# Edge loops of a graph kernel in trips of two iterations, extra sums for every second group, eight raw groups

## The reference

```python
def _gcn(x, W, b, src, dst, w, n):
    h = x @ W
    agg = jax.ops.segment_sum(w[:, None] * h[src], dst, num_segments=n)
    return agg + b

h = _gcn(f1, W1, b1, src, dst, values, N)
root1 = f1[root_idx[batch]]
x = _leaky(jnp.concatenate([h, root1], axis=1))
x = _leaky(_gcn(x, W2, b2, src, dst, values, N))
root2 = f2[root_idx[batch]]
x = _leaky(jnp.concatenate([x, root2], axis=1) @ Wl + bl)
```

## Time and profile before

| | |
|---|---|
| Median of three runs | 2652.09 us (2641.73 to 2658.28) |
| Profiled execution, its own time | 2650.82 us |
| Its span | 2649.1 us |
| Mean granted clock of PE | 0.84 |
| First layer's edge loop with node steps (first to last stage) | 110.8 to 1268.0 us |
| Second layer's | 1334.2 to 2574.8 us |

### The profile page before, as it was taken

How to read it: one execution, slowest core, us unless ns; L and a number is a source line. 1 busy time by engine, 2 the same in 40 slices (tenths; PEclk the granted TensorE clock), 3 DMA queues, 4 the chain that set the end, 5 groups by cost and what they waited for, 6 DMA issues and landing times.

```text
span 2649.1 us, 39172 instructions
## 1 busy us (share of the span) xinstructions
PE 1820.2 (69%) x7140; PEld 1432.8 (54%) x7141; DVE 1141.4 (43%) x3987; ACT 375.1 (14%) x939; POOL 1507.6 (57%) x1580
## 2 busy tenths in 40 slices
PE   0476656666656666565478788888878778777886
PEld 0354445444444444444256666666657566565664
DVE  6443333333333332333245445455444444444456
ACT  5200000000000000000011111111211112111121
POOL 3566565666566666665555556565656655666620
PEclk9988788877777678777678899998889888898887
DMA  7733233333233333332222222222222222222312
GB/s 240 234 91 88 85 89 87 89 89 91 87 89 95 93 87 97 93 95 83 80 72 73 77 81 81 77 83 81 81 77 81 85 81 79 81 81 83 87 32 97
DMA packets 113292, 242.23 MB, mean 91 GB/s; under 512 B 28934, under 2 KB 62661, under 8 KB 113259
## 3 DMA queue, kind: packets, MB, share of 16 engines
q0 software_dynamic: 75200, 205.10, 27.0%
q1 hardware_dynamic: 30094, 29.04, 3.4%
q10 hardware_dynamic: 7964, 7.76, 0.9%
HBM read 222.42 MB, written 19.38 MB: 91 GB/s over the span
## 4 chain that ended last, share of the span: by engine, by line
PE 28%; issue 26%; DVEq 19%; DVE 16%; another core or an unknown queue 8%; ACT 2%; DMA 1%; POOL 0%; ACTq 0%
PE ps_agg L573 17%; DVE S L942 6%; PE ps_dn L678 4%; DVEq L942 3%; PE ps_up L689 3%; DVE acc L950 2%; DVEq L964 2%; DVE S_more L942 2%; DVEq L973 2%; DVEq L950 2%; DVEq L977 1%; DVEq L948 1%; DVEq L986 1%; DVEq L949 1%
## 5 line engine op out<-in xcount | busy, mean ns | idle before, releaser
L573 PE MATMUL ps_agg<-ring,S 128*128 x3136 | 886.7, 433 | 377.5 <-DVE acc L950 278.4
L326 POOL DMA_INDIRECT ring<-conv_rows,idx x782 | 755.7, 966 | 537.6 <-DVEq L972 294.9
L326 POOL DMA_INDIRECT ring<-normed_rows,idx x760 | 725.5, 955 | 484.9 <-DVEq L972 231.6
L573 PEld LDWEIGHTS ps_agg<-ring,S 128*128 128x128 f32 x3136 | 663.1, 218 | 544.1 <-issue 442.3
L942 DVE TENSOR_SCALAR S<-iota,dstc,wc 128x128 f32<-128x128 int16 x1584 | 457.8, 354 | 310.5 <-issue 286.8
L950 DVE TENSOR_TENSOR acc<-acc,ps_agg x490 | 206.3, 421 | 872.3 <-remote 421.0
L573 PE MATMUL ps_agg<-ring,S_more 128*128 x768 | 254.2, 488 | 264.8 <-DVE S_more L942 175.7
L573 PEld LDWEIGHTS ps_agg<-ring,S_more 128*128 128x128 f32 x768 | 179.2, 244 | 328.7 <-issue 298.6
L678 PE MATMUL ps_dn<-fw2s,hT 128*128 128x256 f32 x848 | 228.3, 428 | 0.0
L678 PEld LDWEIGHTS ps_dn<-fw2s,hT 128*128 128x128 f32 x848 | 177.7, 216 | 49.3 <-issue 22.0
L689 PE MATMUL ps_up<-xnT,fw1s 128*128 128x256 f32 x800 | 190.5, 392 | 4.3 <-ACT hT L443 4.3
(11 more groups left out here) (195 smaller groups left out, 1026.0 us busy)
## 6 DMA issues: line engine op xcount, KB each, us to landing
ring<-conv_rows,idx POOLq DMA_INDIRECT x782
ring<-normed_rows,idx POOLq DMA_INDIRECT x760
xs<-in_x SPq DMA_DIRECT2D x6, 1280.0 KB
conv_rows<-rows ACTq DMA_DIRECT2D x50, 128.0 KB
out_rows<-xs SPq DMA_DIRECT2D x6, 896.0 KB
normed_rows<-xs SPq DMA_DIRECT2D x4, 1280.0 KB, 5.2
xs<-in_x SPq DMA_DIRECT2D x4, 1152.0 KB
normed_rows<-xs SPq DMA_DIRECT2D x1, 1152.0 KB, 4.8
```

The lines of the kernel that those rows point to most:

```text
L326: pool.indirect_dma_start(out=ring[:, slot * TG + t, :], out_offset=None, in_=rows_of, in_offset=bass.IndirectOffsetOnAxis(ap=idx[:, tile: ...
L573: last = nc.tensor.matmul(to, select[:, t, :], moving, start=(t == 0), stop=(t == TG - 1))
```

## The change

- **Trips of two.** One iteration (`first_turn`, `edge_round` with b = 0) stands ahead of the loop, and the loop makes 24 trips of two iterations. The two halves of the ring, the PSUM bank, and the places of S are then constants of the code. Semaphores are one for each group of an iteration (`s_ready[q]`, `mm_done[q]`, `acc_done[q]`) and count iterations, so that their values are the same for all four groups. The four table entries of an iteration are read together. DVE copies the iteration's columns of destinations and weights to `cols`, from where S is made without a computed address.
- **Extras for every second group.** Extras of groups 0 and 1 are done in one loop behind group 1, those of 2 and 3 behind group 3: on PE after the piece of the node step, on DVE before it. They use bank 0, and DVE waits in this loop for PE's matmuls. Groups 0 and 2 on PE wait until the extra's sum is added (`x_added`).
- **POOL** waits once for eight gathers (`acc_done[q + 1]`), not once for four.
- **The start.** RAWG is 8: the whole ring (30 tiles) is gathered raw. POOL normalises 14 tiles of the input's rows and 14 of the raw tiles, ACT 35 and 16. The tables are computed before the rows' statistics, the first edge iteration runs before the root's term, and the rows' stores go ahead of the weights' loads on SP. The last node step of the first layer stands behind the loops.

```diff
-    RAWG = 6
+    RAWG = 8
...
-        dstc = sb("dstc", [P, PADT + NT])
-        wc = sb("wc", [P, PADT + NT])
-        dmore = sb("dmore", [P, TG])
+        dw = sb("dw", [P, 2, PADT + NT])
+        dstc = dw[:, 0, PADT:PADT + NT]
+        cols = sb("cols", [P, 2, 2, RING])
+        xcols = sb("xcols", [P, 2, TG])
...
-        XCH = [(39, NW), (29, 39), (20, 29), (10, 20), (0, 10)]
+        XCH = [(39, NW), (29, 39), (19, 29), (14, 19), (7, 14), (0, 7)]
+        BY_POOL = range(4, len(XCH))
...
-        s_ready = [sem(f"s_ready{l}") for l in L2]
-        more_ready = [sem(f"more_ready{l}") for l in L2]
-        mm_done = [sem(f"mm_done{l}") for l in L2]
-        acc_step = [sem(f"acc_step{l}") for l in L2]
-        group_used = [sem(f"group_used{l}") for l in L2]
+        s_ready = [sem(f"s_ready{q}") for q in range(QG)]
+        mm_done = [sem(f"mm_done{q}") for q in range(QG)]
+        acc_done = [sem(f"acc_done{q}") for q in range(QG)]
+        first_cols, cols_ready = sem("first_cols"), sem("cols_ready")
+        x_copied, x_ready, x_done, x_added = sem("x_copied"), sem("x_ready"), sem("x_done"), sem("x_added")
...
                     if l == 0 and g == RAWG:
+                        pool.wait_ge(stats_ready, 2)
+                        for c in BY_POOL:
+                            for w in range(*XCH[c]):
+                                last = nc.gpsimd.tensor_scalar(xs[:, X0 + w, :], xs[:, X0 + w, :], rstd[:, w:w + 1], nmr[:, w:w + 1], ALU.mult, ALU.add)
+                            last.then_inc(f_pool, 1)
+                        pool.wait_ge(raw_stats, 1)
+                        for t in RAW_TILES[0]:
+                            last = nc.gpsimd.tensor_scalar(ring[:, t, :], ring[:, t, :], raw_rstd[:, t:t + 1], raw_nmr[:, t:t + 1], ALU.mult, ALU.add)
+                            if t % TG == TG - 1 or t == RAW_TILES[0][-1]:
+                                last.then_inc(raw_first, 1)
                         for stored in f_stored:
                             pool.wait_ge(stored, 16)
-                    if g >= SLOTS:
-                        pool.wait_ge(group_used[l], g - SLOTS + 2)
+                    if it >= 2 and q % 2 == 0:
+                        pool.wait_ge(acc_done[q + 1], it + NIT * l)
...
             zero(NW // 2, NW)
+            zero(0, NW // 2)
             normalise_rows(0)
-            zero(0, NW // 2)
             normalise_rows(1)
-            normalise_raw(0)
-            for stored in f_stored:
-                act.wait_ge(stored, 16)
-            act.wait_ge(root_ready, 1)
-            r = within(act.value_load(rooti[0:1, 2:3]), N - 1)
-            act.dma_start(rootcol[:, :], f_dram[ds(r, 1), :].rearrange("o (k p) -> p (k o)", p=P)).then_inc(rootcol_loaded, 16)
-            normalise_raw(1)
+            act.wait_ge(raw_stats, 2)
+            for t in RAW_TILES[1]:
+                last = nc.scalar.activation(ring[:, t, :], ring[:, t, :], ACT.Identity, scale=raw_rstd[:, t:t + 1], bias=raw_nmr[:, t:t + 1])
+            last.then_inc(raw_second, 1)
...
+            def sums(bank, select, moving):
                 for t in range(TG):
...
+                    last = nc.tensor.matmul(ps_agg[:, bank, 0:D], select[:, t, :], moving(t), start=(t == 0), stop=(t == TG - 1))
+                return last
+            def group(q, b, n, gathered):
+                added = within(pe.snap(items), ITEMS, 1) if q % 2 == 0 else None
+                pe.wait_ge(landed[b][q], gathered[q])
+                pe.wait_ge(s_ready[q], n(0))
+                pe.wait_ge(acc_done[(q + 2) % QG], n(0 if q < 2 else 1))
+                if q % 2 == 0:
+                    pe.wait_ge(x_added, added)
+                sums(q & 1, S[:, q, :, :], lambda t: ring[:, b * RING + q * TG + t, :]).then_inc(mm_done[q], 1)
+            def more_sums(q, b, n, spans):
+                first, count = spans
+                with pe.If(0 < count):
+                    with pe.Fori(0, count) as j:
+                        i = within(pe.snap(items), ITEMS, 1)
+                        second = within(pe.snap((j + (SLOT + 1) - first) >> CBITS), 1)
+                        at = within(pe.snap(second * TG + (b * RING + (q - 1) * TG)), SLOTS * TG - TG)
+                        pe.reg_mov(items, i + 1)
+                        pe.wait_ge(acc_done[q - 1], n(1))
+                        pe.wait_ge(x_ready, i)
+                        pe.wait_ge(x_added, i)
+                        sums(0, S_more, lambda t: flat(ring[:, t:SLOTS * TG - TG + 1 + t, :][:, ds(at, 1), :])).then_inc(x_done, 1)
+            def turn(b, n, row, gathered, steps=None, step=None):
+                _, entries = nc.values_load_multi_w_load_instructions(
+                    wtab[0:1, ds(row, QG)], engines=(mybir.EngineType.PE,), min_val=0, max_val=ENTRY, skip_runtime_bounds_check_because="the tables it comes from hold clamped values")
+                more = [within(pe.snap(v >> CBITS), NW - 1) for v in entries]
+                spans = {q: (more[q - 1], within(pe.snap(more[q - 1] + more[q]), 2 * NW - 2)) for q in (1, 3)}
+                for q in range(QG):
+                    group(q, b, n, gathered)
+                    if steps:
+                        steps[q](*step)
+                    if q in spans:
+                        more_sums(q, b, n, spans[q])
...
+                turn(1, n, row, [odd] * QG, steps, step[0])
+                n2 = Count(pe, n(1))
+                row2 = within(pe.snap(m * (-2 * QG) + QG * (NIT - 3)), NG - QG)
+                turn(0, n2, row2, [even] * (QG - 1) + [short], steps, step[1])
...
-            def select(ready, to, dst_of, tile):
+            half, step = dve.alloc_register("dve_half_lag"), dve.alloc_register("dve_step")
+            items, pend = dve.alloc_register("dve_items"), dve.alloc_register("pending_slot")
+            def select(ready, to, of):
 
                 for t in range(TG):
-                    column = within(dve.snap(tile + t), PADT + NT - 1)
-                    at = dstc[:, ds(column, 1)] if dst_of is None else dst_of[:, t:t + 1]
-                    last = V.tensor_scalar(to[:, t, :], iota[:, 0:P], at, wc[:, ds(column, 1)], ALU.is_equal, ALU.mult)
+                    last = V.tensor_scalar(to[:, t, :], iota[:, 0:P], of[:, 0, t:t + 1], of[:, 1, t:t + 1], ALU.is_equal, ALU.mult)
                 last.then_inc(ready, 1)
 
-            def add_last(l, i):
...
+            def add(slot, bank, done):
+                to = flat(acc[:, ds(slot, 1), :])
+                V.tensor_tensor(to, to, ps_agg[:, bank, 0:D], op=ALU.add).then_inc(done, 1)
+            def add_group(q, n, slot):
+                added = within(dve.snap(items), ITEMS, 1) if q % 2 else None
+                dve.wait_ge(mm_done[q], n(0))
+                dve.wait_ge(acc_done[(q - 1) % QG], n(0 if q == 0 else 1))
+                if q % 2:
+                    dve.wait_ge(x_added, added)
+                add(slot, q & 1, acc_done[q])
+            def add_pending(n):
+                add_group(QG - 1, Count(dve, n(-1)), within(dve.snap(pend), A0 + NW - 1, A0))
+            def more_sums(q, n, col, slots, spans):
+                first, count = spans
+                with dve.If(0 < count):
+                    with dve.Fori(0, count) as j:
+                        i = within(dve.snap(items), ITEMS, 1)
+                        dve.reg_mov(items, i + 1)
+                        second = within(dve.snap((j + (SLOT + 1) - first) >> CBITS), 1)
+                        mask = within(dve.snap(second * SLOT), SLOT)
+                        down = within(dve.snap(j - (first & mask)), NW - 1)
+                        tile = within(dve.snap(second * TG + (col + (q - 1) * TG)), PADT + NT - TG)
+                        below = within(dve.snap((slots[q - 1] & (mask * -1 + SLOT)) + (slots[q] & mask)), A0 + NW - 1, A0)
+                        slot = within(dve.snap(below - 1 - down), A0 + NW - 1, A0)
+                        V.tensor_copy(xcols[:, 1, :], dw[:, 1, ds(tile, TG)])
+                        V.tensor_scalar(xcols[:, 0, :], dw[:, 0, ds(tile, TG)], shifts[:, ds(down, 1)], None, ALU.add).then_inc(x_copied, 1)
+                        dve.wait_ge(x_copied, i)
+                        select(x_ready, S_more[:, :, :], xcols)
+                        dve.wait_ge(x_done, i)
+                        dve.wait_ge(x_added, i)
+                        dve.wait_ge(acc_done[q - 1], n(1))
+                        add(slot, 0, x_added)
+            def edge_round(l, n, b, row, col, steps=None, s=None):
+                if not isinstance(row, int):
+                    add_pending(n)
+                if steps:
+                    dve.wait_ge(acc_done[QG - 1], n(0))
+                    dve.sem_inc(window_ready[l], 1)
+                _, entries = nc.values_load_multi_w_load_instructions(
+                    wtab[0:1, ds(row, QG)], engines=(mybir.EngineType.DVE,), min_val=0, max_val=ENTRY, skip_runtime_bounds_check_because="the tables it comes from hold clamped values")
```

(20 more changed lines are left out.)

464 lines of the change are left out of this document (227 added, 237 removed).

## The result

The changed kernel is **slower**: 2837.57 us (median of four runs, 2811.31 to 2847.92) against 2648.45 us, a ratio of 1.070 (95% interval 1.061 to 1.078). The forecast was 2363 us. The profiled execution took 2834.91 us.

A forecast was written before the change was run, and what follows sets the result against it. It took register, branch and semaphore instructions, slowed to 0.7 us during long gather runs, to bound the edge loops. Terms -130 - 121 - 12 - 25 = -288 took 2650.8 us to 2363 us; 8-in-10 range 2185 to 2530.

The forecast's parts named there:

- the price of the slow stretches: Edge loops: in long gather runs each non-computing instruction costs DVE and PE some 0.7 us instead of 0.07.
- 13 slow instructions: First layer: some 13 instructions of 0.69 us form the path during about 9 of an iteration's 24.1 us.
- The term for POOL's wait for eight gathers: POOL's release wait: halves the waits, makes each later by one group; at worst 3.0 us pause behind every eight.
- The extras: Second layer: DVE stands at extras behind PE's FFN piece, delaying normalisation and zT; 24 x 1.6 = +38 us.
- Rival D: Second layer's extras behind the FFN piece make the kernel slower: 2810 us, or 2760 in a smaller form; chance 0.05.
- Its smaller form: Edge loops: POOL pauses 3.0 us behind every eight gathers, giving 26 us an iteration and 2760 us.
- Its larger form: Second layer: each of 48 extras exposes FFN piece and normalisation, 6.8 + 3.3 us, together 485 us; 2810 us.
- Rival C: Loop jumps: the sums' unnamed waits, 5.2 us each, are the price of a trip; halved trips give 2408 us; chance 0.07.
- Rival A: Edge loops: POOL sets the pace throughout, 20.3 and 21.0 us an iteration, 2194 us; chance 0.22.
- The start: Before the first stage: less ACT work, earlier stores and more gathers inside POOL's wait save 12 us.
- Between the layers: Gap between layers: without register instructions between matmuls PE and DVE can follow POOL, saving 25 us.
- Two iterations in 40 us instead of 57: Gap between layers: PE and DVE following POOL do two iterations this fast; the basis given for -25 us.

The follow-up runs named there:

- g1: Changed kernel with three of four gathers left out behind the first eight groups of each layer: 1888.53 us.
- g2: Kernel before with three of four gathers left out behind the first eight groups of each layer: 1796.76 us.
- e2: Kernel before with one edit, POOL waiting once for eight gathers: 2890.2 us, ratio 1.082.
- m2: Kernel before with POOL waiting once for eight gathers, measured again in another sitting: 2894.1 us, ratio 1.083.
- m3: Kernel before with ring places given back one group later, in a sitting with stalls: 2670.61 us, ratio 0.999.
- n4: Kernel before with ring places given back two groups later: 2652.49 us, ratio 1.001.
- n5: Kernel before with ring places given back three groups later: 2638.96 us, ratio 0.997.
- m1: Changed kernel unchanged, measured again in another sitting: 2889.14 us, ratio 1.079.
- e1: Changed kernel, but POOL waits once for each group of four gathers instead of eight: 2768.65 us, ratio 1.034.
- k1: Kernel before with ring places given back one group later, in the sitting without stalls: 1.003 of the kernel before's 2109.29 us.
- m4: Kernel before with a memset and a wait for its end behind each four gathers, in a sitting with stalls: 2678.83 us, ratio 1.002.
- e3: Changed kernel, but PE does the extras ahead of the node step's piece: 2916.17 us, ratio 1.091.
- e4: Changed kernel with POOL waiting for each group of four gathers and PE's extras ahead of the node step's piece: 2726.06 us, ratio 1.021.
- e5: Changed kernel, but DVE does its piece of the node step ahead of the extras: 2888.39 us, ratio 1.078.
- f1: Changed kernel with POOL waiting for each group of four gathers, plus a memset and wait behind each group: 2719.69 us, ratio 1.018.

## Why the prediction was wrong

- **The step that failed: the price of the slow stretches was put on the number of register instructions.** The rows were read rightly as far as they go: such instructions take 0.7 us during a run of gathers. But removing them (740 became 51) did not shorten the stall; the engine reached the next wait sooner and stood there, mostly until POOL's run ended ("remote": 241 to 526 us in the first layer). That a stall mostly ends behind POOL's run stood in the earlier trace rows already: the chain resumed at 764.01, in POOL's pause from 761.39. I took the resumption as relief for slow instructions, and it was the end of the stall itself. g1 and g2 show the rest: without POOL's load this work is off the path. The prediction's 13 slow instructions on the path of a first-layer iteration were too many as well: the trace has 6.4 of DVE and 2.9 of PE.
- **The term for POOL's wait for eight gathers was set to nothing; alone it costs 8%** (e2, m2: +216 and +225 us). The prediction said that it "takes away half of the waits and makes each later by one group". Lateness is free (m3, n4, n5). What costs is the grain: each release now starts a run of at least eight, and most stalls last until the run is over. The prediction's own model made stalls grow with the run, but took runs of eight as the good case that the change would bring nearer; the kernel before has 51 runs of four and none of 16, the changed one none of four and 54 of 16.
- **The extras** were forecast at +38 us in the second layer, against a gain of 159. g1 against g2 measures +87 for the loop without POOL's load, and PE waits for bank 0's sum (49.3 us of the 700), hardly for zT (7.6). Under load, without the wait for eight (e1), the second layer is 1.6 us an iteration slower, 77 us.
- **The parts don't add.** On the kernel before the wait for eight costs 8%; with it, the rest of the change is worth between 0 and -1% (m1 against m2 in one sitting, the first measurement against e2 in two). Without it, the rest costs 3.4% (e1). In the first layer the rest gains 1.5 to 1.8 us an iteration under long stalls (26.8 to 25.0 and 25.4), in the second it loses 0.8 to 1.4.
- **Rival D** named the sign and nearly the number (2810 and 2760 us), with 0.05. Its smaller form, POOL pausing behind every eight gathers, is the place that the runs bear out, but it had 3.0 us a pause where 7.0 were measured, and it did not have the reason, the stall that lasts as long as the run; that the number is near is luck. Its larger form, 10 us exposed for each extra, is not borne out: 1.8 us are, for an iteration with one extra in the mean. It should have had more weight, since the forecast relied on a model of stalls whose onset no row fixed.
- **Rival C** is out: with half the jumps the first layer's unnamed waits of sums rose from 46 to 72, and under the cut it takes 13.98 against 13.95 us an iteration. The Trainium skill's rule on taken branches ("Runtime: NRT & Kernel Launch", Instruction fetch mechanics) shows no price in these two.
- **Rival A** is what the kernel before does where there are no stalls: 2109 us. Whether the changed kernel would be near it there was not measured; no run of it fell in that sitting.
- **The start** was -7.5 us for -12 in the two profiles compared, but that is no more than the spread of profiles (last section); POOL's normalising was done at 80.4 us, not at 61. Between the layers the 25 us did not come. That gap is 36 us in the sitting without stalls (k1) and 64 to 66 in the profiles of the two kernels compared here, so it is stall, not register work.
- **Two sums of the prediction** don't add up, and change nothing in its outcome. "Two iterations in 40 us instead of 57" are 17 us, and the term was 25. Rival D's 26 us an iteration give 2749 us with no other term, not 2760.

What makes an engine's signals late during a run of gathers stays open. The runs show that it comes and goes between sittings with the same kernel. They do not show whether that is the chip or its state: the last sitting (n4, n5) was on a chip of the same number as the one of k1, and had stalls.

## What to carry to other kernels

When engines stop and go on together, look for what they resume with (here mostly the end of POOL's run) before you price what they were executing when they stopped. A wait that is made coarser to save instructions also makes the work behind it come in larger pieces: try that edit by itself, as one line on the old kernel. And measure a kernel that leans on many indirect gathers in more than one sitting, for a fifth of its time may belong to where and when it ran.

## What was not expected of the hardware

- The same kernel takes 2109 us in one sitting and 2644 to 2675 us in the five others. In the first, POOL's gathers follow each other at 1.25 us through whole layers (20 us an iteration) without disturbing the other engines.
- In the others, PE's finished work becomes known to DVE and ACT late while POOL gathers, in the stretch above by 12 and 13 us (1923.8 and 1922.1 to 1935.5), and both go on within 0.2 us of each other, 3 us after the run's end. Behind a run of eight this takes 1.6 us, behind one of 24 it takes 4.0.
- Whether the new start is worth anything is not shown. The first stage comes at 110.8 us in the profile of the kernel before, but at 101.2, 105.7, 106.1, 110.7, 103.6 and 100.1 us in e2, m2, m3, m4, n4 and n5, which start in the same way; in the changed kernel and those made from it (e1, e3, e4, e5, f1, m1) it comes at 103.3 to 106.6 us. POOL's tensor_scalar takes 0.54 us a tile (7.54/14), where the prediction took 0.49, and the estimate from the Trainium skill ("GPSIMD Engine Reference", Elementwise) was 0.56. It starts at 63.26, since it waits for the statistics, which the prediction left out:

```profile
63.26 7.54 POOL L352 TENSOR_SCALAR xs<-xs,S_more 128x256 f32<-128x256 f32 x14 [16.37 <-DVEq L952]
```
